# The last unit's aggregation gathered in one place, with part of w2's product ahead of the last tile, and the logits' correction moved to the third unit

## The reference, cut to what matters

```python
x = L0_attn_u                                   # 4 x 1024 tokens x 1024 features
xn = layernorm(x)
s = attn(xn)      # gate product xn @ gate_w, a mean over 1024 tokens, a cumulated decay
# ffn(xn):
p = softmax(xn @ wr.T)                          # 8 experts; the two greatest, shares g1, g2
h = silu(xn @ w1.T)
h = silu(h @ w3.T)
h = h @ w2.T
for k in range(2):
    out = out.at[indices[:, k]].add(gates[:, k:k+1] * h)    # indices are 0..7
g = silu(out)
x = x + s * g
```

## Time and profile before

| | |
|---|---|
| median of 3 runs | 739.27 us (738.48 to 739.31) |
| the profiled execution | 739.49 us, of which the span is 737.7 us |
| PE busy | 727.9 us (99%), 4134 matmul instructions |
| DVE busy | 517.1 us (70%) |
| ACT busy | 356.1 us (48%) |
| POOL busy | 19.8 us (3%) |
| chain that ended last | PE 92%, DVE 4%, DMA 1%, issue 1% |

### The profile page before, as it was taken

One profiled execution on the slowest core, in us unless ns is written; L12 is line 12 of the kernel. 1 busy time (PEld: TensorE's weight loads), 2 busy tenths in 40 slices (PEclk: granted clock), 3 DMA queues, 4 the chain that ended last, 5 costly groups with the idle time before them and its releaser, 6 DMA issues.

```text
span 737.7 us, 9945 instructions
## 1 busy us (share of the span) xinstructions
PE 727.9 (99%) x4134; PEld 601.0 (81%) x4134; DVE 517.1 (70%) x501; ACT 356.1 (48%) x442; POOL 19.8 (3%) x37
## 2 busy tenths in 40 slices
PE   9999999999999999999899999999999999999997
PEld 7888888888888888887788888888888888888885
DVE  5798466758675776589979996663678756895422
ACT  6489658154655765445634543234244442463221
POOL 0001010001010010000000000000000000000000
PEclk9999999999999999999999999999999999999999
DMA  9536944588455848868577803270038103300230
GB/s 328 238 128 215 320 165 157 208 275 279 121 203 194 263 135 293 280 221 296 204 268 241 311 4 142 87 256 1 17 131 309 58 1 143 142 2 0 91 142 3
DMA packets 30941, 126.76 MB, mean 172 GB/s; under 512 B 4592, under 2 KB 4784, under 8 KB 23728
## 3 DMA queue, kind: packets, MB, share of 16 engines
q1 hardware_dynamic: 21648, 109.33, 42.0%
q10 hardware_dynamic: 9248, 16.80, 6.2%
HBM read 105.04 MB, written 37.78 MB: 194 GB/s over the span
## 4 chain that ended last, share of the span: by engine, by line
PE 92%; DVE 4%; DMA 1%; issue 1%; SPq 1%; ACT 0%; DVEq 0%
PE main L902 29%; PE main L904 29%; PE main L903 29%; PE lgp L951 2%; DMA wl6f<-wB 1%; PE lgp L964 1%; PE spare L964 1%; PE main L975 0%; DVE bc L1032 0%; SPq L501 0%; DVE x3f L1032 0%; DVE x3r L1032 0%; DVE x1r L1032 0%; DVE x8f L1032 0%; DVE wl6f L1032 0%
## 5 line engine op out<-in xcount | busy, mean ns | idle before, releaser
L1032 DVE TENSOR_TENSOR s<-s,main 128x512 f32<-128x512 f32 x72 | 48.6, 683 | 69.2 <-PE main L904 69.2
L1032 DVE TENSOR_TENSOR u<-u,main 128x512 f32<-128x512 f32 x36 | 24.1, 682 | 33.9 <-PE main L904 33.9
L760 ACT ACTIVATE s<-main 128x512 f32<-128x512 f32 x36 | 20.7, 594 | 49.7 <-PE main L904 28.2
L785 ACT ACTIVATE rows<-rows 128x512 f32<-128x512 f32 x16 | 10.0, 632 | 65.7 <-DVE rows L1032 65.7
L1032 DVE TENSOR_TENSOR u<-s,main 128x512 f32<-128x512 f32 x32 | 21.7, 684 | 26.3 <-PE main L904 26.1
L721 ACT ACTIVATE rows<-rows,nm 128x1024 f32<-128x1024 f32 x32 | 36.9, 1153 | 1.0
L719 ACT ACTIVATE rows<-rows 128x1024 f32<-128x1024 f32 x32 | 33.5, 1047 | 2.3 <-DMA rows<-x 2.1
L785 ACT ACTIVATE s<-s 128x512 f32<-128x512 f32 x24 | 15.0, 630 | 38.8 <-DVE s L1032 38.8
L785 ACT ACTIVATE u<-u 128x512 f32<-128x512 f32 x24 | 15.0, 628 | 36.3 <-DVE u L1032 36.3
L1032 DVE TENSOR_TENSOR rows<-s,main 128x512 f32<-128x512 f32 x16 | 10.8, 686 | 22.0 <-PE main L904 22.0
L903 PE MATMUL main<-x7r,wh2r 128*128 128x512 f32 x48 | 18.7, 389 | 0.0
(11 more groups left out here) (646 smaller groups left out, 2375.5 us busy)
## 6 DMA issues: line engine op xcount, KB each, us to landing
rows<-x SPq DMA_DIRECT2D x32, 512.0 KB, 4.5
out<-x SPq DMA_DIRECT2D x31, 512.0 KB, 10.2
H_d<-u ACTq DMA_DIRECT2D x32, 256.0 KB, 5.0
bc<-mv_d SPq DMA_DIRECT2D x8, 512.0 KB, 4.4
H_d<-s ACTq DMA_DIRECT2D x16, 256.0 KB, 4.5
rows<-w SPq DMA_DIRECT2D x8, 512.0 KB, 4.6
rows<-xh_d SPq DMA_DIRECT2D x16, 256.0 KB, 5.3
w2f<-w2T SPq DMA_DIRECT2D x2, 2048.0 KB, 10.1
```

Of the source, the lines that this page charges most:

```text
L760: eng.activation(s1[:, j, :], bk, ACT.Copy).then_inc(s_pa, 1)
L785: eng.activation(c, c, ACT.Silu).then_inc(s_sl, 1)
L1032: return eng.tensor_tensor(o, a, b, op)
```

## The change

Three things are done. (1) The correction of the logits moves to unit 3, point (4, 1). The sums of wr no longer come from a DVE reduction and two matmuls: wr's 8 rows are one more job of ACT's row sums (at (1, 3) of unit 3; the job that stood at (1, 2) goes to (1, 1)), SP writes the 8 sums to DRAM at (2, 0) and reads them back to all partitions at (3, 0). The scratch of the correction is in `lg` instead of `bcs[1]`. (2) In units 4 and 5, `x_sum` 3 moves from (1, 0) to (1, 1), behind `low(n, 2)`, as in the other units. (3) In unit 8 all aggregates of products 1, 4 and 5, those of product 6's first two tiles, and three of the eight steps of w2's product go to (6, 2). The tiles (5, 3) and (6, 3), which share a bank, are made in two halves of 256 columns in two banks; the last one's halves are evicted, activated, aggregated and turned one after the other, the eviction's additions on DVE and silu on ACT.

```diff
-JOBS = [(u, r) for u in (2, 3, 0, 1) for r in range(KT)] + [("w1", r) for r in range(KT)]
+JOBS = [(u, r) for u in (2, 3, 0, 1) for r in range(KT)] + [("wr", 0)]
+JOBS += [("w1", r) for r in range(KT)]
...
+LAST = (NN - 1, 6, 3)
+SPLIT = ((NN - 1, 5, 3), LAST)
+SIDES = (slice(0, HT // 2), slice(HT // 2, HT))
...
-            + [(3, *at) for at in ((0, 1), (0, 3), (1, 2), (2, 2), (3, 0), ...
+            + [(3, *at) for at in ((0, 1), (0, 3), (1, 1), (1, 3), (2, 2), (3, 0), ...
...
+        side = [main[bank[LAST]][:, SIDES[0]], lgp[0][:, SIDES[1]]]
...
+            def sums_out():
+                job_done(on, JOBS.index(("wr", 0)))
+                eng.dma_start(sw_d, wrs[0:E, :]).then_inc(s_sws, 16)
+
+            def sums_back():
+                on.wait_ge(s_sws, 16)
+                eng.dma_start(sw[:, :], sw_d.rearrange("e o -> (o e)").partition_broadcast(P)).then_inc(s_swl, 16)
...
+                if n == GATE - 1 and at == (2, 0):
+                    sums_out()
+                if n == GATE - 1 and at == (3, 0):
+                    sums_back()
...
+                if of == "wr":
+                    eng.activation(buf[0:E, :], buf[0:E, :], ACT.Copy, accum_out=wrs[0:E, :]).then_inc(s_st2, 1)
...
-            evict(NN - 1, 6, 3)
+            for e in range(2):
+                on.wait_ge(s_eh, e + 1)
+                eng.activation(s1[:, 3, SIDES[e]], s1[:, 3, SIDES[e]], ACT.Silu).then_inc(s_sh, 1)
...
+            def in_sides(n, i, j):
...
+                for e in range(2):
+                    if e and i == 6:
+                        on.wait_ge(s_pv, pv(NN - 1, 5, 3))
+                    for k in range(4):
+                        ins = three(side[e], xh[:, k, js], xl[:, k, js], wh[:, k, SIDES[e]], wl[:, k, SIDES[e]],
+                                    i == 5 and k == 0, i == 6 and k == 3)
+                    if e:
+                        ins.then_inc(s_mm, 1)
+                    elif i == 6:
+                        ins.then_inc(s_mh, 1)
...
+            def aggregate_side(e):
+                n, i, j = LAST
+                o, h = OUT_OF[i]
+                on.wait_ge(s_sh, e + 1)
+                if e:
+                    on.wait_ge(s_ft, 2)
+                for q in range(NQ):
+                    ins = eng.matmul(acc[o][Q * q:Q * (q + 1), 2 * Q * e:2 * Q * (e + 1)].rearrange("p (k i) -> p k i", i=Q),
+                                     Pz[:, 8 * SOURCE[n] + 4 * h + j, :], in_group(s1[:, j, :], q)[:, 2 * e:2 * e + 2, :],
+                                     start=False, stop=True, skip_group_check=e == 1)
+                return ins
...
-                        on.wait_ge(s_one, 1)
-                        on.wait_ge(s_sw, 1)
-                        eng.matmul(wr_sums, ones, wrs[:, :], start=True, stop=True).then_inc(s_wm, 1)
...
-                if n == NN - 1 and at == (5, 1):
-                    for i in (1, 4):
+                if n == NN - 1 and at == (6, 2):
+                    for i in (4, 5, 1):
                         aggregate(n, i, range(4)).then_inc(s_ph, 1)
-                if n == NN - 1 and at == (6, 1):
-                    aggregate(n, 5, range(4)).then_inc(s_ph, 1)
-            aggregate(NN - 1, 6, range(3))
-            last_product(0, (4, 5))
-            aggregate(NN - 1, 6, range(3, 4)).then_inc(s_ph, 1)
-            last_product(1, (6, 7))
-            last_product(2, range(4)).then_inc(s_fm, 1)
+                    aggregate(n, 6, range(2))
+                    last_product(0, (4, 5, 6))
+            aggregate(NN - 1, 6, range(2, 3))
+            aggregate_side(0).then_inc(s_ph0, 1)
+            last_product(0, (7,))
+            aggregate_side(1).then_inc(s_ph, 1)
+            last_product(1, (0, 1))
+            last_product(2, (2, 3)).then_inc(s_fm, 1)
...
-                on.wait_ge(s_wm, 1)
+                on.wait_ge(s_swl, 16)
                 on.wait_ge(s_mv, len(MV))
-                on.wait_ge(s_ln, LN[(GATE - 1, "d")])
...
-                    part_ = rest[:, 4 * s:4 * s + 4, :]
-                    link(tt(part_, mean, wr_sums.unsqueeze(1).to_broadcast([P, 4, E]), ALU.mult))
+                    part_ = piece(lg[:, 0:P], 32 * s, 4, E)
+                    link(tt(part_, mean, sw[:, :].unsqueeze(1).to_broadcast([P, 4, E]), ALU.mult))
...
-                        sums_of_wr()
...
+                if n == GATE - 1 and at == (4, 1):
+                    logits_normalized()
...
-                if n in (GATE, L2) and at == (1, 0):
-                    x_sum(n, 3)
                 if at == (1, 1):
                     low(n, 2)
-                    if n not in (GATE, L2):
-                        x_sum(n, 3)
+                    x_sum(n, 3)
...
-                        logits_normalized()
                         two_greatest()
...
-                if n == NN - 1 and at == (6, 2):
-                    aggregate_turned(1)
-            evict(NN - 1, 6, 3)
-            aggregate_turned(0)
+                if n == NN - 1 and at == (6, 3):
+                    aggregate_turned()
+            for e in range(2):
+                last_evicted(e)
+            for e in range(2):
+                side_turned(e)
```

More of the change, by code:

```diff
@@ L144 @@
 FOLD = counts(*((n, b) for n in FOLDED for b in "acbd"))
-PH = counts(*((n, i) for n in range(L2, NN) for i in (1, 4, 5, 6)))
+PH = counts(*((n, i) for n in range(L2, NN - 1) for i in (1, 4, 5, 6)), *((NN - 1, i) for i in (4, 5, 1, 6)))
 GX = counts(*((i, j) for i in OUT_OF for j in range(4)))
@@ L152, with program @@
 PART = counts(*((b, k) for b in "ac" for k in range(PIECES[b])))
-def program(nc, x, xT, xa, wB, w11, w1, w2T, small, out):
+def program(nc, x, xT, xa, wB, w11, w1, wr, w2T, small, out):
     loads, loaded = {}, [0] * PLACES
@@ L218, in program @@
         ws = sb("ws", [P, KT])
-        wrs = sb("wrs", [P, E])
+        wrs = sb("wrs", [P, 1])
+        sw = sb("sw", [P, E])
         hb = sb("hb", [P, KT])
@@ L291, in program @@
         s_s = sem("s_s")
-        s_sw = sem("s_sw")
-        s_wm = sem("s_wm")
+        s_sws = sem("s_sws")
+        s_swl = sem("s_swl")
         s_fd = sem("s_fd")
@@ L296, in program @@
         s_mm = sem("s_mm")
+        s_mh = sem("s_mh")
+        s_eh = sem("s_eh")
+        s_sh = sem("s_sh")
+        s_ph0 = sem("s_ph0")
         s_pa = sem("s_pa")
@@ L495, in row @@
                 of, r = JOBS[q]
-                r0 = r * P if of == "w1" else BATCH[of] * SEQ + r * P
-                eng.dma_start(job_buf(q), (w1 if of == "w1" else x)[r0:r0 + P, :]).then_inc(s_row[q % 2], 16)
+                if of == "wr":
+                    src = wr
+                elif of == "w1":
+                    src = w1[r * P:(r + 1) * P, :]
+                else:
+                    r0 = BATCH[of] * SEQ + r * P
+                    src = x[r0:r0 + P, :]
+                eng.dma_start(job_buf(q)[0:E, :] if of == "wr" else job_buf(q), src).then_inc(s_row[q % 2], 16)
+            def sums_out():
[4 more added lines that the diff above has]
+                eng.dma_start(sw[:, :], sw_d.rearrange("e o -> (o e)").partition_broadcast(P)).then_inc(s_swl, 16)
             def first_block(b, k):
@@ L941, in product @@
                 ins.then_inc(s_mm, 1)
+            def in_sides(n, i, j):
+                xh, xl = xr(n, f"h{i}"), xr(n, lo_place(n, i))
+                wh, wl = w_r(i, 0), w_r(i, 1)
+                js = slice(j * P, (j + 1) * P)
+                bank_free(on, n, i, j)
+                w_in(on, layer_of(n), i)
+                x_in(on, n, i)
+                on.wait_ge(s_yt, 1)
+                for e in range(2):
[8 more added lines that the diff above has]
+                        ins.then_inc(s_mh, 1)
             def logits(n, b):
@@ L984, in _ @@
                 at = (p, j)
-                product(*tile_of(t))
+                if tile_of(t) in SPLIT:
+                    in_sides(*tile_of(t))
+                else:
+                    product(*tile_of(t))
                 if n == 0:
@@ L1231, in evict @@
                     on.wait_ge(s_pv, pv(n, 3, j))
+                if (n, i, j) in SPLIT:
+                    tt(dst[:, SIDES[0]], old[:, SIDES[0]], side[0], ALU.add)
+                    tt(dst[:, SIDES[1]], old[:, SIDES[1]], side[1], ALU.add).then_inc(s_pv, 1)
+                    return
                 tt(dst, old, bk, ALU.add).then_inc(s_pv, 1)
@@ L1345, in attention, with aggregate_turned, side_turned, last_evicted @@
                 eng.transpose(yt[:, :, :].rearrange("p k e -> p (k e)"), y[:, :, :].rearrange("p k e -> p (k e)")).then_inc(s_yt, 1)
-            def aggregate_turned(o):
-                on.wait_ge(s_ph, PH[(NN - 1, 5 if o else 6)])
+            def aggregate_turned():
+                on.wait_ge(s_ph, PH[(NN - 1, 5)])
                 on.wait_ge(s_oz, 1)
-                eng.transpose(o32[:, 4 * o:4 * o + 4, :].rearrange("p k e -> p (k e)"), acc[o][:, 0:P]).then_inc(s_ft, 1)
+                eng.transpose(o32[:, 4:8, :].rearrange("p k e -> p (k e)"), acc[1][:, 0:P]).then_inc(s_ft, 1)
```

(15 more changed lines are left out.)

13 lines of the change are left out of this document (7 added, 6 removed).

## The result

Before takes 739.29 us (738.48 to 740.18), the changed kernel 734.29 (733.17 to 734.73): 5.0 us less, a ratio of 0.993 with a 95% interval of 0.9913 to 0.9947. The forecast was 734.4, in the range of 733.1 to 737.0. The profiled execution took 734.73 us, with a span of 732.0 where before had 739.49 with 737.7: the spans are 5.7 us apart, the times of these two 4.8, since 2.7 us lie around the span after and 1.8 before.

The account below looks back on a forecast made before the run. PE was taken as nearly always busy, its longest wait 3.0 us for DVE's x3r. The terms -4.85 - 0.03 + 0 + 0 made -4.9 us, from the median of 739.27 to 734.4 us, range 733.1 to 737.0.

Parts of the forecast that it names:

- The hole and its clock: Unit 4, PE ahead of product 2: removing the wait for x3r saves 3.16 us, the lower clock behind it 1.69.
- The spare times: Unit 4 after the moves: 1.9 us to spare at product 2, 1.1 us at tile (4, 4, 1).
- Where the correction went: Unit 3 at (4, 1): the added DVE and ACT work and the read-back of wr's sums cost PE nothing.
- Unit 0: Dropping two L992 matmuls frees 0.21 us of PE, lost ahead of product 4: 0, bounds -0.2 and 0.
- The end: Unit 8's merged block and the work behind the last tile: nearly the same PE work, -0.03 us, no gain.
- T: End of the last main tile on PE, 728.35 before; ACT's last silu forecast 3.25 us behind it.
- the halves: Tiles (5, 3) and (6, 3) as 48 matmuls of 256 columns: 0.1134 us each, cost 0, bounds 0 and 3.7 us.
- the balance: Unit 8's end: 1.74 us moved ahead, 0.33 for one block saved, 3.25 behind the last tile against 4.69: -0.03.
- The sum: Whole kernel: -4.85 - 0.03 + 0 + 0 = -4.9 us, giving 734.4 us.
- the sides' full price: Unit 8's end: aggregating instructions of 64 columns priced like 128, 0.027 us each; at half, 0.2 us less.

Follow-up runs that it names:

- the old end on the new middle: Changed kernel with whole tiles, blocks of aggregates at (5, 1) and (6, 1) and w2's product as before: 733.6 us, ratio 0.9929.
- the kernel with the other widths: Changed kernel with product 2 of unit 8, tiles j=1 to 3, made as 384 + 128, 256 + 256 and four times 128 columns: 737.39 us, ratio 0.9979.

## Why the prediction was right, point by point

- **The hole and its clock.** Forecast 3.16 + 1.69 = 4.85 us; the middle gave 4.88 between marks of the profiles, 4.87 by the old end on the new middle. The mechanism is shown; that the size fits so closely is no separate proof, since both numbers rest on the same profiled execution of before, and its 1.69 is one draw (0.08 of it is the slower first matmul, 1.6 the clock). x3r was to end at 347.4 and ended at 347.16.
- **The spare times.** 1.9 us forecast at product 2, 1.75 measured; 1.1 forecast at (4, 4, 1), 1.2 measured. Both places turned into waits when DVE was delayed by 1.8 us, and no other did in unit 4. x2r and x3r were to arrive together at 345.1. Here ACT's x2r was done at 341.93 + 1.91 = 343.84, a full microsecond ahead of x3r. It stands behind an eviction that waits for a store H_d, as in the earlier trace rows, and that store happened to land earlier (the eviction starts at 341.44, in before at 342.66). In the eight profiles of kernels with this order on DVE, x2r is done between 1.2 us ahead of the start that the queue leaves x3r and 0.1 behind it; in the kernel with the other widths x3r started 0.1 us late for it, and PE did not feel that. In four of the eight the two arrive within 0.2 us of each other, as forecast. x6r waited for x8f to 349.39 (forecast 349.6) and nobody felt it.
- **Where the correction went.** PE has no wait in unit 3, and none at the read-back of the sums, as forecast.
- **Unit 0.** Forecast 0, bounds -0.2 and 0; the profile shows 0.22 at PE's product 4 (54.13, has 54.35). I do not put it down to the two matmuls of L992: the twelve profiles of kernels with the same instructions there have that matmul at 53.58 to 54.89, so the scatter between executions is larger than the term.
- **The end** is the step that was mis-sized, -0.03 forecast, +0.22 measured. ACT's last silu came at T + 3.23 (728.16 - 724.93), forecast T + 3.25, but by two errors that cancel: a side's 64 columns cost half (8 instructions in 725.37 - 725.26 = 0.11 us, 726.18 - 726.05 = 0.13 for the other), and PE idled 0.24 us for ACT, not 0.1. The failed term is that the halves "cost the same, 0.1134 each", which gave the halves 0: they cost 0.31. With it the balance is 1.74 - 0.33 + 3.25 - 4.69 + 0.31 = +0.28. Measured, PE needs 724.93 - 444.71 = 280.22 us from unit 5's mark to T, where before needs 728.35 - 449.81 = 278.54: 1.68 more (forecast 1.41, with the halves 1.72), and 4.69 - 3.23 = 1.46 less behind T.
- **The sum.** -4.88 + 0.22 = -4.66 between the marks where I had -4.9. Two terms are not in the forecast at all. What lies between the silu and the span's end takes 4.65 us in before's one profile and 3.83 to 3.85 in all twelve of the changed kernels, -0.8; with unit 0's -0.22 that makes the spans' 5.7. Outside the span lie 1.8 us in before and 2.0 to 3.0 in the four executions of the kernel after, where the forecast took 1.8 for both. The two nearly cancel, and no run shows the cause of either. That 734.4 meets 734.29 to 0.1 us is luck.
- **Two rules of the Trainium skill.** The Trainium skill ("TensorE: Matmul & The Clock Gate", The mechanism; the prediction names the section behind it) has a line by which a load overlaps a running matmul only where the row group differs. The runs speak against that line: with all rows in use 512, 256 and 128 columns went 0.227, 0.120 and 0.111 us apart. For the sides' full price the prediction leaned on the floor of some 25 ns from start to start that the Trainium skill gives ("TensorE: Matmul & The Clock Gate", Back-to-back issue gap). It does not hold for these small matmuls in column groups. The 0.027 of the earlier trace rows is a mean: in the trace of before four instructions start within 0.02 us and the next four 0.109 after the first ones. A side's 8 of 64 columns go in the same way, the second four 0.056 behind the first, 0.014 each in the mean.

## What to carry to other kernels

Where one engine is busy 99% of the time, a long wait can be worth more than its length (here 3.2 us of hole, and 1.6 of clock in the profiled execution), and the cure is in the order of the queue that feeds it: take out of that queue whatever is not wanted soon, then look for the next place with the least spare time, which one delay of known size finds. Work of the busy engine that is moved ahead of a final barrier gains nothing by itself; it pays for every turn into and out of the stream and uncovers the latency that it used to hide. Leaving it in one stretch behind the barrier was 0.9 us faster than the cleverer order with its halves. And where two profiles explain a difference of a few microseconds, the spread over executions (here of the clock and of what lies outside the span) says how much of a close match is chance.

## What the hardware showed that I had not expected

Full-array loads of 128x128 weights go 0.111 us apart though each lasts 0.19, and matmuls of 256 columns 0.120. The first matmul behind a wait is 0.30 to 0.33 us from the next one at full clock, against 0.227 in the stream. Holes of 0.5 to 1.0 us left the granted clock at 1.00, at the level of 2.4 GHz, in the stretch behind them, and no execution of those kernels has a mean under 0.999. Behind the hole of 3.2 us eight matmuls ran at the 1.2 GHz level in both profiles, from 0.6 to 1.2 us after PE had resumed; but 15 of the 57 executions of these two kernels beside the experiments have spans some 2 us shorter, 11 of them at a mean clock of 1.000, so such a hole does not cost it every time. Where between 1.0 and 3.2 us it begins was not tried.
